# Graph kernel on one Trainium2 core: degree sums in two levels, sum windows of 96 nodes, and more runs of 32 tiles without gathers

## What is computed

```python
# src, dst: [100000], sorted by dst;  edge_attr_128: [100000, 128]
def gcn_conv(x, src, dst, ew, W, b):            # self-loops added
    deg = segment_sum(ew, dst)
    dinv = where(deg > 0, rsqrt(deg), 0.0)
    norm = dinv[src] * ew * dinv[dst]
    return segment_sum((x @ W)[src] * norm[:, None], dst) + b

h = relu(gcn_conv(x, src, dst, ew, W1, b1))
h = sigmoid(gcn_conv(h, src, dst, ew, W2, b2))
x = layernorm(x + h)

z, rh = x @ fc_w.T, edge_attr_128 @ fc_r_w.T
e = leaky_relu(z[src] @ aw[0] + z[dst] @ aw[1] + rh @ aw[2])
alpha = segment_softmax(e, dst)
out = relu(segment_sum(alpha[:, None] * (z[src] + rh), dst) + z @ loop_w)
x = layernorm(x + out)
```

## Time and profile before

| what | value |
|---|---|
| time, median of 3 runs | 2410.56 us |
| span of the profiled execution | 3348.6 us |
| TensorE busy in it | 2044.2 us (61%) |
| VectorE busy | 1834.8 us (55%) |
| ScalarE busy | 946.7 us (28%) |
| GpSimd busy | 1718.9 us (51%) |
| mean granted TensorE clock | 0.787 |
| 16 DMA engines, gathers / hardware queues | 14.8% / 15.8% of their span |

### The profile page before, as it was taken

One profiled execution on the slowest core, in us unless ns is written; L12 is line 12 of the kernel. 1 busy time (PEld: TensorE's weight loads), 2 busy tenths in 40 slices (PEclk: granted clock), 3 DMA queues, 4 the chain that ended last, 5 costly groups with the idle time before them and its releaser, 6 DMA issues.

```text
span 3348.6 us, 40819 instructions
## 1 busy us (share of the span) xinstructions
PE 2044.2 (61%) x13384; PEld 1762.3 (53%) x13384; DVE 1834.8 (55%) x7005; ACT 946.7 (28%) x1754; POOL 1718.9 (51%) x1781
## 2 busy tenths in 40 slices
PE   1416444588888911177777888106677667756786
PEld 1315433566767811166666677005666666645675
DVE  3626435577779810156656687217654564546457
ACT  1316000122233300033333444101254225412541
POOL 7351666665550067466556500555766646663640
PEclk9857667798999955588988899557778778877888
DMA  4112221222221122123333332525343534443431
GB/s 118 30 42 66 69 61 47 61 61 63 60 62 32 51 76 53 41 74 86 99 103 102 93 91 80 138 62 147 97 103 97 134 93 102 108 117 79 103 97 34
DMA packets 272093, 270.54 MB, mean 81 GB/s; under 512 B 43454, under 2 KB 218709, under 8 KB 271862
## 3 DMA queue, kind: packets, MB, share of 16 engines
q1 hardware_dynamic: 201790, 143.87, 15.1%
q0 software_dynamic: 56640, 117.52, 14.8%
q10 hardware_dynamic: 13448, 6.47, 0.7%
HBM read 254.14 MB, written 13.97 MB: 80 GB/s over the span
## 4 chain that ended last, share of the span: by engine, by line
PE 35%; DVE 21%; another core or an unknown queue 21%; issue 15%; ACT 4%; SPq 1%; DMA 1%; POOL 1%; ACTq 0%; DVEq 0%; POOLq 0%
PE ps L858 9%; PE ps L910 8%; DVE SR L1608 5%; PE ps L860 3%; PE ps L898 3%; PE ps L1045 2%; DVE U L1709 2%; DVE SR L1681 2%; DVE SR L1571 1%; PE ps L885 1%; DVE U L1648 1%; PE ps L1029 1%; POOL ring L720 1%; PE ps L792 1%
## 5 line engine op out<-in xcount | busy, mean ns | idle before, releaser
L720 POOL DMA_INDIRECT ring<-x_d,srcC x1132 | 1109.7, 980 | 971.2 <-issue 579.0
L858 PE MATMUL ps<-SR,ring 128*128 128x128 f32 x3540 | 672.5, 320 | 205.0 <-issue 132.0
L858 PEld LDWEIGHTS ps<-SR,ring 128*128 128x128 f32 x3540 | 580.5, 231 | 238.9 <-issue 178.9
L720 POOL DMA_INDIRECT ring<-h_d,srcC x494 | 469.9, 951 | 457.1 <-DMA h_d<-Lb 170.9
L1681 DVE TENSOR_SCALAR SR<-iota_r,cols 128x288 f32<-128x288 f32 x735 | 365.0, 564 | 303.9 <-remote 226.6
L910 PE MATMUL ps<-SR 128*128 128x288 f32 x1470 | 416.6, 435 | 118.1 <-ACT SR L1232 75.3
L910 PEld LDWEIGHTS ps<-SR 128*128 128x128 f32 x1470 | 292.3, 205 | 212.7 <-ACT SR L1232 77.5
L860 PE MATMUL ps<-SR 128*128 128x128 f32 x1564 | 340.3, 312 | 40.8 <-issue 34.6
L1232 ACT COPY SR<-ps 128x512 f32<-128x512 f32 (+1 forms) x195 | 106.0, 561 | 758.4 <-remote 502.9
L860 PEld LDWEIGHTS ps<-SR 128*128 128x128 f32 x1564 | 279.6, 228 | 48.3 <-issue 48.0
L898 PE MATMUL ps<-rows,SR 128*128 128x128 f32 x1470 | 196.2, 285 | 122.5 <-ACT SR L1241 90.6
(11 more groups left out here) (288 smaller groups left out, 2703.4 us busy)
## 6 DMA issues: line engine op xcount, KB each, us to landing
SR<-in_edge_attr_dram SPq DMA_DIRECT2D x97, 512.0 KB
SR<-low_d SPq DMA_DIRECT2D x90, 256.0 KB
U<-dlo_d SPq DMA_DIRECT2D x74, 256.0 KB
ring<-x_d,srcC POOLq DMA_INDIRECT x1132
ring<-h_d,srcC POOLq DMA_INDIRECT x494
SR<-dlo_d SPq DMA_DIRECT2D x12, 512.0 KB
ring<-in_edge_attr_dram SPq DMA_DIRECT2D x12, 512.0 KB
U<-lo_d SPq DMA_DIRECT2D x18, 256.0 KB
```

What stands on the lines that cost most here:

```text
L720: pool.indirect_dma_start(ring[:, ring_at(p, h if p < 2 else q), k, 0:width], None, (x if p == 0 and h < R0 else table)[:, :], bass.Indire ...
L858: last = nc.tensor.matmul(ps[(p * NA + k) % 2][:, at], ring[:, ring_at(p, h), j, 0:D], S[:, gg % NS, j, :], start=False, stop=stop)
```

## The change

- **Windows:** W goes from 128 to 96, in all three passes, and with it SPAN from 376 to 344. The one-hots of a tile and the matmuls of lines 858 and 860 have 96 columns. (The tiles keep a pitch of 128 in SR.)
- **Runs:** ten sets instead of nine, on other banks; pass 0 has seven runs, pass 1 ten. Pass 0 then gathers 558 tiles in 70 steps, pass 1 462 tiles in 58. CHUNK_AT puts the 91 chunks of pass 0 at steps 23 to 66 (78 chunks at 29 to 68 before) and the 130 of pass 1 at steps 1 to 53 (117 at 1 to 57 before). The ten sets are made from step 11 to 65 of pass 0 (nine from 17 to 69 before). Pass 2 has three runs as before, the third on another set number over the same tiles.
- **Degrees:** the window is split in 7 high numbers and 16 low ones. Three VectorE instructions over 56 tiles build the high one-hot (392 elements), the low one-hot (896) and the high one-hot times the three weight parts (1176); 14 such chunks replace the 584 and 198 single ones, and ScalarE has no part left. TensorE does 806 matmuls of 128 x 21 with 16 rows of output; three reductions (VectorE) and eight small matmuls give the columns. Nine more instructions of 784 elements make the numbers, six of them behind the ranks.
- **Start:** R0 is 12 instead of 18: 96 tiles come from x, and POOL waits for x1 after them. `find_odd` runs behind the last degree chunk. Ten constant-setting instructions move ahead of the wait for the rest of src, and the vector products of the weights move behind the second and fourth chunk.

```diff
-W = 128
+W = 96
...
-R0 = 18
+R0 = 12
...
+DL = 16
+DH = W // DL + 1
+DT = 7 * GT
+DEG = [range(t, min(t + DT, T)) for t in range(0, T, DT)]
+DB = BW // 3
+NH = NP // DL
...
-SETK = (6, 8, 10, 12, 14, 15, 2, 4, 9)
-USED = ((0, 1, 2, 3, 4, 5), (6, 7, 0, 1, 8, 2, 3, 4, 5))
+SETK = (6, 8, 10, 11, 12, 14, 15, 2, 3, 5)
+USED = ((0, 1, 2, 3, 4, 5, 6), (7, 8, 9, 0, 1, 2, 3, 4, 5, 6))
...
-CHUNK_AT = [[29 + m * 40 // (N0 * NC) for m in range(N0 * NC)], [1 + m * 57 // (len(USED[1]) * NC) for m in range(len(USED[1]) * NC)]]
-MAKE = [17 + 6 * i for i in range(NSET)]
-MAKE_STEP = (0, 1, 3, 4)
+CHUNK_AT = [[23 + m * 44 // (N0 * NC) for m in range(N0 * NC)], [1 + m * 53 // (len(USED[1]) * NC) for m in range(len(USED[1]) * NC)]]
+MAKE = [11 + i * 51 // (NSET - 1) for i in range(NSET)]
+MAKE_STEP = (0, 1, 2, 3)
...
-            for q in range(G):
-                if q in DEG_ACT:
-                    pe.wait_ge(s("deg_onehot_act"), 2 * DEG_ACT.index(q) + 2)
-                else:
-                    pe.wait_ge(s("deg_onehot"), DEG_DVE.index(q) + 1)
...
+            for c, ts in enumerate(DEG):
+                pe.wait_ge(s("deg_onehot"), c + 1)
...
+                for j, t in enumerate(ts):
+                    for k, lo, hi, h0 in deg_pieces(t):
+                        last = nc.tensor.matmul(ps[5 + k][0:DL, 3 * lo:3 * hi], degL[:, c % 2, j, :],
+                                                degW[:, c % 2, j, h0:h0 + hi - lo, :].rearrange("p h k -> p (h k)"), start=False, stop=t == DEG_LAST[k])
                 last.then_inc(s("deg_summed"), 1)
...
+            pe.wait_ge(s("deg_rows"), 1)
+            for j in range(P // DL):
+                last = nc.tensor.matmul(ps[2][:, 0:NB], lift[:, P - DL - DL * j:2 * P - DL - DL * j], deg16.rearrange("l (b j) -> l j b", j=P // DL)[:, j, :],
+                                        start=j == 0, stop=j + 1 == P // DL)
...
-                        last = nc.tensor.matmul(ps[(p * NA + k) % 2][:, at], ring[:, ring_at(p, h), j, 0:D], S[:, gg % NS, j, :], start=False, stop=stop)
+                        last = nc.tensor.matmul(ps[(p * NA + k) % 2][:, at], ring[:, ring_at(p, h), j, 0:D], S[:, gg % NS, j, 0:W], start=False, stop=stop)
...
-            for q in DEG_DVE:
-                if q >= ND:
-                    dve.wait_ge(s("deg_summed"), q - ND + 1)
-                for j, t in enumerate(tiles(q)):
-                    last = v.tensor_scalar(SH[:, q % ND, j, :], iota_h[:, :], rankC[:, t:t + 1], None, ALU.is_equal)
-                last.then_inc(s("deg_onehot"), 1)
-                if q == 0:
+            for c, ts in enumerate(DEG):
+                n, at = len(ts), slice(ts[0], ts[-1] + 1)
+                if c >= 2:
+                    dve.wait_ge(s("deg_summed"), c - 1)
+                v.tensor_tensor(degH[:, c % 2, 0:n, :], iota_h[:, 0:DH].unsqueeze(1).broadcast_to([P, n, DH]),
+                                highC[:, at].unsqueeze(2).broadcast_to([P, n, DH]), ALU.is_equal).then_inc(s("dve_step"), 1)
+                steps[0] += 1
+                v.tensor_tensor(degL[:, c % 2, 0:n, :], iota_h[:, 0:DL].unsqueeze(1).broadcast_to([P, n, DL]),
+                                lowC[:, at].unsqueeze(2).broadcast_to([P, n, DL]), ALU.is_equal)
+                dve.wait_ge(s("dve_step"), steps[0])
+                v.tensor_tensor(degW[:, c % 2, 0:n], degH[:, c % 2, 0:n, :].unsqueeze(3).broadcast_to([P, n, DH, 3]),
+                                ewP[:, at, :].unsqueeze(2).broadcast_to([P, n, DH, 3]), ALU.mult).then_inc(s("deg_onehot"), 1)
+                if c == 0:
                     weights()
-                if q == 2 * ND:
-                    find_odd()
+                    low_numbers()
+                if c == 3:
+                    vectors()
+            find_odd()
+            dve.wait_ge(s("deg_summed"), len(DEG))
```

More of the change, by code:

```diff
@@ L53, in tiles, with deg_pieces @@
     return range(q * GT, min((q + 1) * GT, T))
[L56 to L73 removed]
+DL = 16
[4 more added lines that the diff above has]
+NH = NP // DL
+def deg_pieces(t):
+    h0, out = base(t) // DL, []
+    for k in range(h0 // DB, (h0 + DH - 1) // DB + 1):
+        lo, hi = max(h0, k * DB), min(h0 + DH, (k + 1) * DB)
+        out.append((k, lo - k * DB, hi - k * DB, lo - h0))
+    return out
+DEG_LAST = [max(t for t in range(T) if any(c[0] == k for c in deg_pieces(t))) for k in range(-(-NH // DB))]
 BA = 3 * P
@@ L817, in _ @@
-            deg_cols(NK - 1)
+            for c, ts in enumerate(DEG):
+                pe.wait_ge(s("deg_onehot"), c + 1)
+                if c == 0:
+                    for k in range(len(DEG_LAST)):
+                        clear(ps[5 + k][0:DL, :], DL)
+                for j, t in enumerate(ts):
+                    for k, lo, hi, h0 in deg_pieces(t):
+                        last = nc.tensor.matmul(ps[5 + k][0:DL, 3 * lo:3 * hi], degL[:, c % 2, j, :],
+                                                degW[:, c % 2, j, h0:h0 + hi - lo, :].rearrange("p h k -> p (h k)"), start=False, stop=t == DEG_LAST[k])
+                last.then_inc(s("deg_summed"), 1)
+                if c == 1:
+                    pe.wait_ge(s("cols_copied"), 7)
+                    pe.wait_ge(s("vectors_made"), 1)
+                    nc.tensor.matmul(ps[0][:, 0:P], a0B, fcw, start=True, stop=True)
+                    nc.tensor.matmul(ps[0][:, P:2 * P], a1B, fcw, start=True, stop=True)
+                    nc.tensor.matmul(ps[0][:, 2 * P:3 * P], a2B, fcrw, start=True, stop=True).then_inc(s("wprod"), 1)
@@ L1135, in wide_row_sum @@
                 for k in range(GT):
-                    last = nc.tensor.matmul(ps[2][:, a * W:(a + 1) * W], tile[:, k, 0:D], S[:, 0, k, :], start=k == 0, stop=k == GT - 1)
+                    last = nc.tensor.matmul(ps[2][:, a * P:(a + 1) * P], tile[:, k, 0:D], S[:, 0, k, :], start=k == 0, stop=k == GT - 1)
                 return last
@@ L1494, in _ @@
             v.tensor_copy(srcC[:, at], got).then_inc(s("cols_copied"), 1)
+            link(v.tensor_scalar(offI, offI, DL - 1, None, ALU.bitwise_and))
             dve.wait_ge(s("dst_loaded"), 16 * (EB + 1))
             v.tensor_copy(dstF, dstR).then_inc(s("dstF_made"), 1)
+            v.tensor_copy(offF, offI)
+            link(v.memset(lift, 0.0))
+            dve.wait_ge(s("ident_made"), 1)
+            v.tensor_copy(lift[:, P - DL:P], ident[0:DL, 0:DL])
+            v.memset(zero_h[:, :], 0.0)
+            v.memset(ones_h[:, :], 1.0)
+            v.tensor_scalar(before[:, :], iota_h[:, :], pidx[:, 0:1], None, ALU.is_gt)
+            v.memset(epsc[:, :], EPS)
+            v.tensor_scalar(negp[:, 0:1], pidx[:, 0:1], -1.0, None, ALU.mult)
+            v.memset(negp[:, 1:2], 1.0)
+            v.memset(rows[:, :, D:XW], 0.0)
+            v.memset(padI[:, 0:DOFF], -1)
+            v.memset(padI[:, DOFF:DOFF + DLEN - DOFF - E], int(FAR))
+            v.memset(s2C[:, T:TC], 0.0).then_inc(s("constants_set"), 1)
             dve.wait_ge(s("src_loaded"), 16 * EB)
@@ L2190, in _ @@
                     with dve.Fori(0, NB) as r:
-                        s1row, mrow = (a[:, bass.ds(r * P, P)].unsqueeze(1).broadcast_to([P, GT, W]) for a in (wideC, wideD))
+                        s1row, mrow = (a[:, bass.ds(r * P, P)].unsqueeze(1).broadcast_to([P, GT, P]) for a in (wideC, wideD))
                         step = g * (5 * NB) + r * 5
```

143 lines of the change are left out of this document (50 added, 93 removed).

## The result

The changed kernel takes 2480.6 us (median), the kernel before 2410.3: ratio 1.029, 95% interval 1.0258 to 1.0321. It is **slower**; the forecast was 2340, in a range that ended at 2395.

What follows compares the result with a forecast made beforehand. GpSimd (POOL) was taken to bound the kernel, TensorE and VectorE close behind. 2410.6 - 80 (fewer gathers) + 20 (pass 1) - 10 (pass 0) = 2340 us, range 2285 to 2395.

Steps and rivals of the forecast that it cites:

- more runs: Added run slots and tenth set: +28 us of TensorE a pass; pass 1 loses 20 us, pass 0 wins 10.
- I take 10 us won: Pass 0: steps 9.8 us over 44 instead of 9.4 over 40, but sums start 60 us earlier; 0 to 22.
- Fewer gathers: GpSimd, passes 0 and 1: 64 tiles less at 1.25 us each, 80 us less, 40 a pass.
- Degrees and start: Start, up to x1: 14 chunks of 3.1 us, setup_done near 83, no wait for x1; 0 us.
- Narrow windows: One-hots and group sums of 96 columns: 0.35 us a step less on VectorE, nothing saved on TensorE.
- (a): GpSimd bounds everything: TensorE's step stays below 10.0 us, by the gap formula losing 16 x 25 ns; 2320, chance 0.15.
- Pass 2, 0: Pass 2 keeps its gathers, narrower one-hots lie beside them: 0 us.
- The account of before: Sum for 2410.6 us: first gather at 5.8, 2212 of gathers, 108 at the end, 85 for hand-overs and trailing.
- (b): The start did cost before, part of 55 us being the wait at x1, now removed; 2295, chance 0.10.
- (c): TensorE bounds passes 0 and 1 from start to end, so nothing is gained; 2410, chance 0.08.
- (d): Slower: (c) with a lower clock, 2433 at a granted 0.75, 2474 at 0.5; chance 0.07 together with (f).
- (f): Degree chunks above 8.8 us, not 3.1, x1 after 206; or slowed gathers, 22 us; chance 0.07 together with (d).

Runs made afterwards that it cites:

- bunched: dw_old_runs with pass 1's 117 chunks laid down three to a step in 39 steps, no instruction more; 2535.8 us, ratio 1.0518.
- dw_old_runs: The changed kernel with the old nine sets, six and nine runs, and old chunk and set places; 2408.8 us, ratio 1.0002.
- slots_16: The changed kernel with 16 buffers for run one-hots in place of 15; 2437.4 us, ratio 1.0121.
- d_only: dw_old_runs with W = 128 in place of 96; 2414.5 us, ratio 1.0031.
- six_nine_early: The changed kernel with the old nine sets and six and nine runs, keeping the early chunk and set places; 2377.1 us, ratio 0.9872.
- before_16: The kernel before with 16 buffers for run one-hots in place of 15, nothing else; 2380.5 us, ratio 0.9888.
- six_nine_16: six_nine_early with 16 buffers for run one-hots in place of 15; 2376.2 us, ratio 0.9866.
- before_again: The kernel before, unchanged, profiled once more; 2408.1 us.
- seven_nine_55: Seven and nine runs from nine sets, early places, with pass 1's 117 chunks over 55 steps in place of 57; 2396.8 us, ratio 0.9961.

## Why the prediction was wrong, point by point

**The step that failed is "more runs", above all "I take 20 us lost" for pass 1.** It compared mean step lengths: 9.25 slots a step, 9.5 us of TensorE, divided by the 0.92 of a clear stretch, 10.3 against GpSimd's 10.0. Measured, pass 1 takes 733 us for 58 steps, 12.6 us a step, and it lost 124 us against the 609 that 649.3 - 40 leaves, where 20 were forecast. Three things went wrong. The mean hides that chunks come whole: 9.25 slots are steps of 8 and of 12, and a step of 12 costs 5.0 us more than one of 8 in the rows shown, not 2.8 (bunched: the same work, 127 us slower). The 0.92 was taken from steps of two chunks and carried over as a constant; the busy share fell to 0.80 (585 of 733 us), in bunched by order alone to 0.76. And the clock was taken at the level of the clear stretches: the prediction had priced the same pass at 0.88 with 74 us lost, and set it aside; the profile gives 0.88 for the pass (0.92 before), so this was the better number. The +28 us of added matmuls were right (29 by the estimate above), and about as much again came with the clock. That lower clock is a result of the crowding, since in bunched order alone brought it down; but it then lengthens the same matmuls, 52 of the 131 us that pass 1 grew there. No run holds the clock fixed, so how much of the rest hangs on it stays open.

**"I take 10 us won" in pass 0** was wrong by 35 us. It rested on the earlier start of the sums. dw_old_runs shows that this start alone brings 0.8 us (818.0 against 818.8); slots_16 shows what held pass 0: the 15 buffers, 26 us of the 35. The tenth set has a part too, not added to it: with seven runs from nine sets pass 0 is 21 us shorter at 15 buffers (783.8 against 804.5), though a bank differs as well. The prediction never looked at NQ. The wait was in the trace that it read, the first profile of the kernel before:

```profile
DVE SR L1681 <- PE ps L910: 77.1, 30, 7.0
```

**Fewer gathers, -80 us:** right, in GpSimd's own finishing times, and all given back as idle time.

**Degrees and start, 0:** right within 7 us (d_only 1.0031), and at nothing with 96 columns; dinv is there at 83.05, where the prediction's 83 + 4 gave 87.

**Narrow windows:** nothing on TensorE is right, 2.00 us for 16 records of 96 columns. 0.35 us a step on VectorE was too much: the eight one-hots take 2.01 us, in place of 2.13. By the gap formula of the Trainium skill (TensorE: Matmul & The Clock Gate, Back-to-back issue gap) the narrow sums would have been cheaper; the trace does not agree, with 2.00 us for 16 records against 2.03 for 128 columns. 32 columns less would be 13 ns a record by it, an estimate (32/2.4), where rival (a) took 25. What they still share, weight load or another floor, no run tells apart. That 96 columns come with a lower clock the prediction did not have.

**Pass 2, 0:** right, 1 us.

**The account of before** had the right sum from wrong parts. Gathers are 1.25 us apart only in unbroken stretches; over a whole pass they are 1.30 (passes 0 and 2) and 1.27 (pass 1), 71 us more for 1770 at their mean of 1.29. The hand-overs hold 68 us, and the end comes 49 after the start of the last gather, not 108. The statement that GpSimd bounds the kernel before stands but for the 30 us or so that other places (six_nine_early) or one more buffer (before_16) bring at the first hand-over: six_nine_16 shows what its limit is at both hand-overs closed, 2376.

**The rivals.** (a) fell with pass 1's mean step of 12.6 us. (b) fell with before_again, which does not wait for x1. (c), TensorE bounding passes 0 and 1, was the right family with 0.08 of the chance, and (d), its slower form, gave 2433 and 2474 by way of the clock. The time of 2474 was near, its condition, a clock of 0.5, was not: 0.867 over the changed kernel's profile and 0.877 before. Its threshold was worked out wrongly: a step of 9.1 us at 0.97 reaches 10.0 at 0.88, not at 0.88 x 0.97. Put right, pass 1 of the changed kernel (0.88) is at it and that of the kernel before (0.92) is not. (f) has a slip as well: with chunks of 8.8 us x1 comes at 107 + 14 x 5.7 = 187, and 206 needs 10.2. Its second half, gathers that slow down beside two-input instructions of VectorE, is borne out: the first 96 stand 1.39 us apart in place of 1.28, 10 us in all, and farther with larger such instructions (1.47 in d_only), without harm to dw_old_runs. That W has no other way to reach those gathers was not tried.

**Still open.** Why 96 columns are 15 us slower than 128 with the new runs (pass 1: 733 against 720, TensorE busy 585 against 569): the lower clock goes with it, and its cause was not tried. Which of VectorE's three waits makes a crowded step dear in pass 1. What the tenth set itself costs in pass 0. And the exact price of a three-chunk step, which came out at 3.6 us from bunched and at 5 us from seven_nine_55.

## What to carry to other kernels

When engines share the work of a step through small rings of buffers, cost the fullest step and its neighbour and not the mean step, and compare the ring with what two neighbouring steps put into it: here 15 buffers stood against 8 + 8. Work taken off the bounding engine should go where the other engines have gaps, and the same work spread over earlier steps brought 32 us, where seven and ten runs in crowded steps lost 72. Price a fuller step at a lower clock too, if the trace has stretches at either. If a profile is far longer than the runs, take another before arguing from its waits.
